# The second attention of a two-layer transformer block: a pair's twelve units in two runs, four and eight

## What is computed

```python
q = rmsnorm(x @ Wq, q_rms_w); k = rmsnorm(x @ Wk, k_rms_w); v = x @ Wv
gate = softplus(einsum('bthd,hd->bht', k, u_n) / sqrt(D))
bias = where(causal, -dist * omega_eff * gate, -inf)
scores = einsum('bihd,bjhd->bhij', q, k) * scale + bias
attn = softmax(scores); y = einsum('bhij,bjhd->bihd', attn, v)
return y.reshape(B, T, H * D) @ Wproj
```

## Time and profile before

| | |
|---|---|
| median of three runs | 2271.55 us (2269.65 to 2274.39) |
| the profiled execution: time, span | 2270.39 us, 2268.6 us |
| TensorE matmuls (PE) | 2053.4 us busy, 91% |
| VectorE (DVE) | 1373.6 us, 61% |
| ScalarE (ACT) | 1157.6 us, 51% |
| GpSimd (POOL) | 843.4 us, 37% |
| DMA | 335.88 MB, 148 GB/s on average |

### The profile page before, as it was taken

The page is one execution under the profiler, slowest core; times in us unless marked ns, Lnnn a source line. Parts: engine busy times, 40 slices in busy tenths (PEclk is TensorE's granted clock), DMA queues, the critical chain, the costliest instruction groups (busy, mean ns, idle before and its releaser), DMA issues.

```text
span 2268.6 us, 34364 instructions
## 1 busy us (share of the span) xinstructions
PE 2053.4 (91%) x11728; PEld 1167.7 (51%) x11728; DVE 1373.6 (61%) x3345; ACT 1157.6 (51%) x1859; POOL 843.4 (37%) x544
## 2 busy tenths in 40 slices
PE   5799999998487879886899999999999999999998
PEld 2333333334476445444566556655666556655644
DVE  4777777774732678875566666666667655333311
ACT  2366666667343667674455555555555543223232
POOL 5000000000601445432577777777777773000000
PEclk8899999999589899996899999999999999999999
DMA  5233333111365579977667766776677677543300
GB/s 178 96 128 129 127 114 127 57 51 59 103 184 146 171 221 323 282 221 203 148 160 178 180 162 157 179 180 164 154 180 179 167 208 186 136 98 84 89 5 10
DMA packets 263468, 335.88 MB, mean 148 GB/s; under 512 B 22828, under 2 KB 185948, under 8 KB 262888
## 3 DMA queue, kind: packets, MB, share of 16 engines
q1 hardware_dynamic: 247992, 305.82, 50.2%
q0 software_dynamic: 7664, 24.39, 3.0%
q10 hardware_dynamic: 7640, 3.48, 0.5%
HBM read 193.69 MB, written 122.62 MB: 139 GB/s over the span
## 4 chain that ended last, share of the span: by engine, by line
PE 42%; issue 6%; DVE 4%; DMA 1%; SPq 0%; ACT 0%; DVEq 0%; ACTq 0%
PE ps L1284 10%; PE ps L953 7%; PE ps L937 6%; PE ps L906 6%; PE ps L938 6%; PE ps L1235 3%; DVE a1mx L1009 2%; PE ps L940 1%; PE ps L1295 1%; PE ps L1272 1%; PE ps L1273 1%; DVE a1mx L1005 1%; DMA a1FQ<-s_q 1%; DVE a1mx L1002 0%; PE ps L909 0%
## 5 line engine op out<-in xcount | busy, mean ns | idle before, releaser
L1120 POOL TENSOR_TENSOR a1sum<-a1sum,a1prob 128x1024 f32<-128x1024 f32 (+3 forms) x256 | 463.8, 1812 | 84.0 <-ACT a1prob L1063 51.2
L1063 ACT ACTIVATE a1prob<-ps 128x512 f32<-128x512 f32 (+2 forms) x640 | 328.0, 553 | 245.8 <-PE ps L940 214.5
L476 DVE TENSOR_REDUCE a0grid<-ps 128x8 f32<-128x1024 f32 x288 | 346.9, 1221 | 116.5 <-PE ps L351 71.9
L1002 DVE CUSTOM_DVE_ANT_0 ps<-ps,c_mask_ij 128x128 f32<-128x128 f32 x496 | 264.4, 551 | 194.3 <-issue 190.0
L577 ACT ACTIVATE a0prob<-ps 128x1024 f32<-128x1024 f32 x288 | 292.6, 1025 | 171.6 <-PE ps L377 91.5
L937 PE MATMUL ps<-a1QA,a1KA 69*128 69x512 f32 (+3 forms) x768 | 285.6, 379 | 5.0 <-DMA a1QA<-a1neg 5.0
L953 PE MATMUL ps<-a1prob,a1V 128*64 128x512 f32 (+3 forms) x1536 | 273.8, 499 | 5.0 <-ACT a1prob L1063 5.0
L938 PE MATMUL ps<-a1QB,a1KB 128*128 128x512 f32 (+3 forms) x768 | 264.3, 352 | 0.0
L906 PE MATMUL ps<-a1KA,a1QA 68*128 68x128 f32 x744 | 225.0, 381 | 4.6 <-DMA a1KA<-s_g 3.8
L953 PEld LDWEIGHTS ps<-a1prob,a1V 128*64 128x64 f32 x1536 | 102.9, 138 | 173.3 <-issue 138.7
L1005 DVE TENSOR_REDUCE a1mx<-ps 128x1 f32<-128x320 f32 x248 | 146.0, 589 | 70.5 <-PE ps L906 67.6
(11 more groups left out here) (267 smaller groups left out, 3196.1 us busy)
## 6 DMA issues: line engine op xcount, KB each, us to landing
a1FQ<-s_q SPq DMA_DIRECT2D x128, 256.0 KB, 7.9
a1KB<-s_k SPq DMA_DIRECT2D x128, 256.0 KB, 8.5
s_xs<-c_zero POOLq DMA_DIRECT2D x19, 1024.0 KB, 8.9
s_q<-mqkT SPq DMA_DIRECT2D x32, 512.0 KB, 3.4
s_v<-mv SPq DMA_DIRECT2D x32, 512.0 KB, 5.8
s_k<-a1KH SPq DMA_DIRECT2D x32, 512.0 KB, 5.0
s_k<-a1KL SPq DMA_DIRECT2D x32, 512.0 KB, 6.0
a1KA<-s_k SPq DMA_DIRECT2D x64, 256.0 KB
```

The costliest lines, as they stand in the source:

```text
L476: dve.tensor_reduce(grid[g % 2][:, :, a:b + 1:b - a], banks(("max", k)), axis=AX.X, op=ALU.max).then_inc(s1_free, 1)
L1002: dve.tensor_tensor_reduce(bank[:, 0:w], bank[:, 0:w], const["mask_ij"][:, BANK - w:BANK], 1.0, LOWEST, ALU.add, ALU.max, mx[:, x % 2, h, ...
L1063: act.activation(weights_of(g, u)[:, group[0]:group[-1] + 1, off:BANK], both(e, u, group), ACT.Exp).then_inc(weighed, 1)
L1120: pool.tensor_tensor(t[:, :, off:BANK], t[:, :, off:BANK], weights_of(g, u)[:, :, off:BANK], ALU.add).then_inc(summed, 1)
```

## The change

A pair's units go in two runs, 0 to 3 and 4 to 11. So the scores of units 4 to 11 stand in one row, with their jobs; then the den job; then the values of all eight units. The turn of the next pair's maxima goes after unit 11, the last (before: 8, in pair 0: 9). VectorE's count of jobs and ScalarE's `row` and `keep_den` follow: both now come after the exponentials of unit 11, the row first.

```diff
-    runs = [range(r, r + TILES) for r in range(0, NU, TILES)]
+    runs = [range(0, TILES), range(TILES, NU)]
...
-    turn_after = lambda g: TURN if g > 0 else TURN + 1
...
-            return [("turn", 1, 0)] + found if u == turn_after(0) else found
+            return [("turn", 1, 0)] + found if u == NU - 1 else found
...
-        if u == TURN and g + 1 < G:
+        if u == NU - 1 and g + 1 < G:
             found.append(("turn", g + 1, 0))
...
-                    if u == 2 * TILES - 1 and g > 0:
+                    if u == NU - 1 and g > 0:
                         d += 1
...
-                    if u == 2 * TILES - 1 and g > 0:
+                    if u == NU - 1 and g + 1 < G:
+                        row(g + 1)
+                    if u == NU - 1 and g > 0:
                         keep_den(g - 1)
-                    if u == turn_after(g) + 1 and g + 1 < G:
-                        row(g + 1)
```

## The result

The changed kernel takes 2456.4 us (2448.2 to 2468.7), the kernel before 2273.0 (2269.7 to 2275.0) beside it: ratio 1.081 [1.078, 1.084], slower by 183 us. The profiled execution took 2451.2 us. The forecast was 2423, range 2340 to 2460.

What follows compares the result with a forecast made beforehand. TensorE was taken to bound the second attention (99.56 of 100 us busy); 24.92 + 3.3 wait + 2.3 clock = 30.5 us a pair, +5.25, times 29 = 152 us, giving 2423 us, range 2340 to 2460.

Steps and rivals of the forecast that it cites:

- Units 0 to 7 and the scores of unit 8: Second attention: TensorE reaches the first maxima product of the pair after next at 13.73 us instead of 18.41.
- The copy keeps its time and lands at 17.0: Second QA<-QB copy on SP's queue: unmoved by the change, landing 17.0 us into its pair, needed at 13.73.
- A wait of 3.3 us, 29 times: TensorE stands before L906 for the copy, 3.3 us (bounds 1.6 to 4.9) in pairs 1 to 29.
- The pair without the wait, 24.92 us: Second attention's pair without the copy's wait: 13.73 + 4.17 + 1.24 + 5.78 = 24.92 us, 0.33 below before.
- Turn, row, sums and stores hidden at the end: End of pair: some 3 us after the turn, hidden under 1 + 5.78 us of product and values.
- The clock, 2.3 us a pair: After each TensorE hole the granted clock falls to 0.50, costing 2.3 us a pair (bounds 0 and 3.3).
- 28 to 31: Sign of being right: a pair of the second attention lasts 28 to 31 us.
- the likeliest case: Second attention: stall with a lower clock, 30.5 us a pair, 2423 us, own range 2385 to 2455; chance 0.80.
- Both holes of this size that I read were followed by 0.50: Evidence for the lower clock: TensorE holes of 2.66 and 3.1 us, each followed by clock 0.50.
- Stall without a lower clock: Rival, second attention: TensorE waits 3.3 us but stays at 1.00; 29 x 2.95 = 86, 2357 us; chance 0.10.
- VectorE becomes the bound: Rival, long run: copy in by 13.7 us, VectorE's backlog adds 0.5 us a pair, 2287 us; chance 0.06.
- Faster: Third rival, second attention: early transfer, VectorE keeps pace; 31 x -0.33 = -10, 2261 us; chance 0.04.

Runs made afterwards that it cites:

- experiment 10: Changed kernel with both QA<-QB copies issued ahead of SP's other loads and the maxima's combination L1009 as a one-input reduction: 2258.5 us, 0.993.
- Experiment 4: Kernel before, with only the turn of the maxima and the row after it moved to unit 11: 2275.0 us, 1.003.
- Experiment 3: Changed kernel with 14 needless matmuls on TensorE ahead of each wait for the copy: 2363.8 us, 1.041.
- experiment 5: Changed kernel with both QA<-QB copies issued ahead of the loads of FQ and KB on SP's queue: 2305.5 us, 1.013.
- experiment 8: Changed kernel with both copies issued early on SP's queue and the turn back after unit 8: 2382.7 us, 1.048.
- experiment 9: Changed kernel with both copies early and two maxima of units 8 to 11 moved to units 0 and 1 of the next pair: 2289.1 us, 1.007.
- experiment 1: Changed kernel with both QA<-QB copies issued on ScalarE's own queue after units 1 and 4: 2437.3 us, 1.074.

## Why the prediction was right, and where it was off

- *Units 0 to 7 and the scores of unit 8*: 13.73 us forecast, 13.8 measured. Right.
- *The copy keeps its time and lands at 17.0*: 17.2. Right, and from its neighbours' rows, since the copy has none. By the Trainium skill's page "DMA: Bandwidth & Descriptors", section "Anatomy of one DMA", whose figure is for GpSimd's path, an estimate put it at 11.6; the trace does not agree here, where the copy is issued by SP and lands near the end of a full train.
- *A wait of 3.3 us, 29 times*: 95.1 us, 3.28 each. Right.
- *The pair without the wait, 24.92 us*: the changed kernel can't show it; experiment 10, without the wait for the copy, shows 24.92. Its parts there are 13.61, 4.15, 1.42 and 5.74 us against 13.73, 4.17, 1.24 and 5.78. Right, each within 0.2; that their sum agrees to the hundredth is luck.
- *Turn, row, sums and stores hidden at the end*: L937's waits for the row are 3.4 us in the whole span. Right. Experiment 4 shows what cover they need: 3.1 us.
- *The clock, 2.3 us a pair*: this is the term that was mis-sized. Experiment 3 gives 3.2 by difference; the changed kernel's own trace gives 31.78 - 24.92 - 3.28 = 3.58 a pair (2.6 to 5.0). With 29 x 1.28 = 37 us it is more than the 33 between 2423 and 2456; against it, pairs 0 and 30, which the sum took as unchanged, are 5 us shorter in all. The lengths were taken from the earlier trace rows, 3.3 and 6.7 us, two single holes elsewhere; here they are 6.8 to 13.7. The price, half of the length, was too high: its own rows give 1.5 us lost of 3.81, 0.40, and in the pair shown 32.51 - 24.92 - 3.33 = 4.3 us are lost in 10.3, 0.41. I had called half of 6.7 the upper bound; it is below the mean. So the pair came to 31.8, outside the 28 to 31 that were to show the prediction right, and 2456 is 1 above the likeliest case's own 2385 to 2455.
- *"Both holes of this size that I read were followed by 0.50"*: the kernel before has one that was not, 2.3 us long and in an earlier layer, which the prediction does not show (columns as in the earlier trace rows); the hole, and the stretch behind it:

```profile
945.80:948.10 2.30, 0.00 (x0) 0.00 (x0) 2.30 (x3) 1.49 (x3) 1.10 (x1) 1.00 0.23 93
948.20:955.00 6.80, 6.80 (x27) 3.78 (x28) 5.98 (x10) 3.90 (x7) 2.02 (x2) 1.00 0.99 310
```

- *The rivals.* "Stall without a lower clock" is experiment 3, 2364 (forecast 2357), had only by filling the hole. "VectorE becomes the bound" was a real second limit, hidden behind the stall: experiment 5, +0.5 us a pair as estimated (from 0.8, the middle between 0 and 1.6, so in part luck), and beyond that the low clock in nine pairs, which its sum had left out. An early copy alone brings this rival, and not the third, to which the prediction gave it. "Faster", 2261, is experiment 10's 2259: it took both conditions that were named, an early transfer and VectorE keeping pace.

What stays open: the split into 91 and 93 us is by difference between two kernels, and experiment 3's filling left some waits of TensorE's matmuls for the copy (from 1200 to 1700 seven, 5.9 us in all); what makes one small hole lower the clock and another not was not settled (below).

## What to carry to other kernels

Before work is moved forward, look for the transfer that its first instruction needs, and place that transfer's landing by its neighbours in the same train. If the transfer is late, issue it ahead of transfers that are needed later; here a queue of its own didn't do it. A hole in TensorE's work each round is to be priced twice, once as the wait and once for the clock (here 3.3 us and 3.2 to 3.6), and behind a removed wait the next engine's backlog is to be worked out before a gain is claimed.

## What the hardware showed that was not expected

- Holes much shorter than those of the earlier trace rows were followed by a granted clock of 0.50: the 1.29 us of experiment 8 in 23 of 29 pairs, and the 0.42 us of experiment 5 (with smaller gaps around it) in 9 of 29. In their profiled executions these were not: experiment 9's two holes of 0.43 and 0.31 us a pair, experiment 4's of 0.50 to 1.09 us at the start of pairs 2 to 30, and one of 2.25 us in experiment 1. So the length of a single hole does not tell; what does is open.
- A combination of two 128x8 tiles took VectorE 1.41 us with two operands, beside a working GpSimd, and 0.17 us as a reduction with one operand of twice the size. The 1.41 us are mostly waiting: in all 31 combinations of the kernel before, the end comes 0.02 to 0.03 us after that of GpSimd's running instruction. Here are GpSimd's two instructions beside the earlier trace rows and the first one's length in ns (it ends at 1253.38, the combination at 1253.40), then the same in pair 0, where GpSimd ends at 1102.91 and the same combination takes only 0.32 us:

```profile
1251.02 4.85 POOL L1120 TENSOR_TENSOR a1sum<-a1sum,a1prob 128x1024 f32<-128x1024 f32 x2
L1120 POOL TENSOR_TENSOR a1sum<-a1sum,a1prob x1: 2356/2356/2356, 1251.0 to 1251.0; 128x1024 f32<-128x1024 f32 x1
...
1100.54 4.32 POOL L1120 TENSOR_TENSOR a1sum<-a1sum,a1prob 128x1024 f32<-128x1024 f32 x2 [3.13 <-ACT a1prob L1063]
L1120 POOL TENSOR_TENSOR a1sum<-a1sum,a1prob x1: 2368/2368/2368, 1100.5 to 1100.5; 128x1024 f32<-128x1024 f32 x1
1102.61 0.32 DVE L1009 TENSOR_TENSOR a1mx<-a1mx,a1mx 128x8 f32<-128x8 f32 x1
```

  The Trainium skill's page "GPSIMD Engine Reference", section "1. Specifications", says that GpSimd shares its SBUF interfaces with VectorE and contends with instructions there that have two SBUF inputs; these rows agree with it.
- The copy of 256 KB took 8.2 us on a queue of its own, as long as on the queue that carries the rest of the train (8.1 us in the changed kernel).
